# Differential attention with the scores computed once: queries on partitions, differences turned for the weighing

## The reference

```python
q1, q2 = _rope(q1, cos, sin), _rope(q2, cos, sin)    # H = 16, DH = 16
k1, k2 = _rope(k1, cos, sin), _rope(k2, cos, sin)    # KV = 4, repeated for 4 heads
s1 = einsum('bhtd,bhsd->bhts', q1, k1) * scale + mask   # causal
s2 = einsum('bhtd,bhsd->bhts', q2, k2) * scale + mask
diff = softmax(s1) - lam * softmax(s2)
out = einsum('bhts,bhsd->bhtd', diff, v)
out = (out - mean) * rsqrt(var + EPS)                # over (tokens, 32) of a head
out = (out * gn_w + gn_b).reshape(B, T, 512) * 0.8
x = layernorm(x + out @ Wo)
gate = sigmoid(max(x @ router_w.T)); e = argmax(x @ router_w.T)
y = silu_mul((gate * x) @ w_gate_up[e]) @ w_down[e] + silu_mul(x @ shared_gate_up) @ shared_down
out = layernorm(x + y)
```

## Time and profile before

| What | Value |
|---|---|
| Median of 3 runs | 820.88 us |
| The three runs | 817.32, 820.88, 823.03 us |
| Profiled execution | 814.82 us, its span 813.1 us |
| Mean granted TensorE clock | 0.964 |
| PE busy in the span | 739.4 us (91%) |
| DVE busy | 474.6 us (58%) |
| ACT busy | 316.3 us (39%) |
| POOL busy | 308.3 us (38%) |

### The profile page before, as it was taken

The page is one execution under the profiler, slowest core; times in us unless marked ns, Lnnn a source line. Parts: engine busy times, 40 slices in busy tenths (PEclk is TensorE's granted clock), DMA queues, the critical chain, the costliest instruction groups (busy, mean ns, idle before and its releaser), DMA issues.

```text
span 813.1 us, 11581 instructions
## 1 busy us (share of the span) xinstructions
PE 739.4 (91%) x4050; PEld 412.9 (51%) x4050; DVE 474.6 (58%) x1052; ACT 316.3 (39%) x584; POOL 308.3 (38%) x263
## 2 busy tenths in 40 slices
PE   7578899999989999998999999999999889999993
PEld 3343334435434444544344445444326559999993
DVE  2756987775576786437667864867325432433432
ACT  2415544354655434255454342654763102111110
POOL 4055821120885121228841211322150034666653
PEclk9879999999989999999899999999999999999997
DMA  4597084202007610120085101700020066877630
GB/s 134 126 351 184 4 191 72 41 29 42 1 26 165 108 35 30 21 46 1 27 175 75 34 29 28 220 2 0 2 85 1 27 204 218 273 266 258 226 119 0
DMA packets 55832, 78.75 MB, mean 97 GB/s; under 512 B 11543, under 2 KB 43037, under 8 KB 53920
## 3 DMA queue, kind: packets, MB, share of 16 engines
q1 hardware_dynamic: 47072, 65.02, 31.1%
q0 software_dynamic: 3824, 6.83, 2.5%
q10 hardware_dynamic: 4880, 6.16, 2.3%
HBM read 58.32 MB, written 22.41 MB: 99 GB/s over the span
## 4 chain that ended last, share of the span: by engine, by line
PE 73%; DVE 14%; DMA 4%; ACT 3%; issue 2%; POOL 2%; SPq 1%; POOLq 0%; DVEq 0%; ACTq 0%
PE pv_ps L1089 16%; PE wide_ps L1173 10%; PE wide_ps L1075 8%; PE s_ps L926 7%; DVE mneg L1506 6%; PE wide_ps L913 5%; PE wide_ps L1059 3%; PE wide_ps L1031 3%; PE s_ps L929 3%; PE s_ps L960 2%; PE misc L1184 2%; PE pv_ps L1184 2%; PE misc L1006 2%; DVE work L1536 2%; PE wide_ps L1064 2%
## 5 line engine op out<-in xcount | busy, mean ns | idle before, releaser
L1506 DVE TENSOR_REDUCE mneg<-s_ps 128x4 f32<-128x512 f32 (+2 forms) x352 | 214.7, 638 | 82.5 <-PE s_ps L926 45.7
L1287 ACT ACTIVATE w_exp<-wide_ps 128x512 f32<-128x512 f32 x320 | 179.0, 602 | 104.7 <-PE wide_ps L1075 103.3
L1089 PE MATMUL pv_ps<-w_exp,work 128*64 128x512 f32 x640 | 177.0, 633 | 1.6 <-POOL w_exp L1419 0.7
L1419 POOL TENSOR_SCALAR_AFFINE_SELECT w_exp<-w_exp 128x1024 f32<-128x1024 f32 x64 | 70.6, 1106 | 263.7 <-ACT w_exp L1287 263.4
L926 PE MATMUL s_ps<-w_exp 96*128 96x128 bf16 (+2 forms) x896 | 130.7, 250 | 22.9 <-DVE mneg L1506 13.7
L1075 PE MATMUL wide_ps<-w_exp 98*128 98x512 bf16 x320 | 122.8, 394 | 4.5 <-ACT w_exp L1287 3.3
L926 PEld LDWEIGHTS s_ps<-w_exp 96*128 96x128 bf16 x896 | 71.8, 100 | 80.3 <-DVE mneg L1506 41.8
L1075 PEld LDWEIGHTS wide_ps<-w_exp 98*128 98x128 bf16 x320 | 31.1, 100 | 141.0 <-ACT w_exp L1287 68.3
L1173 PE MATMUL wide_ps<-tables,w_exp 128*128 128x128 f32 x736 | 87.6, 278 | 0.0
L1173 PEld LDWEIGHTS wide_ps<-tables,w_exp 128*128 128x128 f32 x736 | 85.7, 195 | 0.1
L1305 ACT COPY work<-pv_ps 128x512 f32<-128x512 f32 x64 | 37.6, 588 | 67.9 <-PE pv_ps L1089 67.3
(11 more groups left out here) (162 smaller groups left out, 922.1 us busy)
## 6 DMA issues: line engine op xcount, KB each, us to landing
w_exp<-w_up_in SPq DMA_DIRECT2D x23, 1024.0 KB, 5.2
w_exp<-q_parts SPq DMA_DIRECT2D x96, 128.0 KB, 5.1
slot_tokens<-x ACTq DMA_DIRECT2D x1, 4864.0 KB, 19.4
work<-x_in SPq DMA_DIRECT2D x8, 512.0 KB, 5.3
w_exp<-w_down_in SPq DMA_DIRECT2D x8, 512.0 KB, 8.7
q_parts<-w_exp SPq DMA_DIRECT2D x6, 512.0 KB, 6.4
w_exp<-k_parts SPq DMA_DIRECT2D x18, 128.0 KB, 4.0
gated_rows<-work SPq DMA_DIRECT2D x4, 512.0 KB, 3.0
```

Of the source, the lines that this page charges most:

```text
L1089: last = nc.tensor.matmul(pv_ps[s * 64:(s + 1) * 64, :], vo[:, kt, g, :], probs[:, (b * NSTEP + n) % NP, s, :], start=(kt == 0), stop=(kt ...
L1287: nc.scalar.activation(probs[:, (b * NSTEP + n) % NP, s], st_bank(v), ACT.Exp, scale=float(DH) ** -0.5).then_inc(st_done, 1)
L1419: nc.gpsimd.affine_select(out=e, in_=e, compare_op=ALU.is_ge, fill=0.0, base=0, pattern=[[0, 8], [1, P]], channel_multiplier=-1).then_inc( ...
L1506: nc.vector.tensor_reduce(out=mneg[:, 1 - own, qt % 2, rows[0]:rows[-1] + 1], in_=s_ps[:, (v - 1) % 2, 0:len(rows) * w].rearrange("p (r k) ...
```

## The change

The scores are computed once. A batch now has 44 groups `GROUPS = (qt, r, heads, g)` in place of 40 steps: in query tile 0 a group is four heads with 128 keys each, in tile 1 two heads with 256, in tiles 2 and 3 one head with 384 and 512; each group has a bank for each of the two maps, with queries on partitions. DVE takes the maxima as before. ACT takes the exponent from the same bank, one instruction per head and map, with the row's negative maximum as bias, and the row sums as a second output (`accum_out`). DVE inverts the sums of map 2 for two groups at once, multiplies them to a `ratio`, and computes the difference of the two maps (`subtract`). PE turns the difference in blocks of 128 (`turn_diff`), ACT copies it out (`take_diff`), and `weigh` multiplies V by it, four groups beside each other in `pv_ps` with 32 rows each. The sum of map 1 is divided out at the end of each query tile (`denom` makes it, `take_out` multiplies). Maxima are no longer turned nor sent; POOL no longer zeroes the diagonal.

PSUM has seven banks in one ring each, four for scores and three for all else, and each bank has its own semaphore `freed`. A step K does the banks of group K, the difference of K - 2, the turning of K - 4, the weighing of K - 8 and the output of K - 10; the order inside a step is `PE_STEP`, `DVE_STEP`, `ACT_STEP`. The attention's output is now kept with dimensions on partitions, so mean and variance come from channel statistics (`stat`, `centre`), and `turn`, `square` and `sum` go. `x2`, the gated rows, the copy of the logits and of the shared expert's sum move from DVE to ACT (`shared_down` adds x2 on PE by an identity matmul). POOL's rotations and additions are issued as four instructions, one for each quarter of the columns. All tasks have new places in the tables. The routed experts' code is unchanged.

```diff
 NEG = -1e30
-NP = 6
+NPROB, NDIFF, NTURN = 4, 3, 6
...
+PER_BANK = [max(1, QT // (qt + 1)) for qt in range(QT)]
+GROUPS = [(qt, r, PER_BANK[qt], g) for qt in range(QT) for r in range(0, 4, PER_BANK[qt]) for g in range(KV)]
+NG, NQUAD = len(GROUPS), len(GROUPS) // KV
+FIRST_G = [min(k for k, x in enumerate(GROUPS) if x[0] == qt) for qt in range(QT)]
+LAST_G = [max(k for k, x in enumerate(GROUPS) if x[0] == qt) for qt in range(QT)]
+
+LAST_QUAD = [LAST_G[qt] // KV for qt in range(QT)]
+NALL = B * NG
+LAG_DIFF, LAG_TURN, LAG_WEIGH, LAG_OUT = 2, 4, 8, 10
...
+put(MIDDLE, 26, "mid", ("choose", 0, 1))
+put(MIDDLE, 26, "end", ("shared_gate", 0, 1))
+put(MIDDLE, 27, "mid", ("rank", 0, 1), ("ids", 0, 1))
+put(MIDDLE, 28, "mid", ("ids", 1, 1), ("ids", 2, 1), ("gate", 0, 1))
+put(MIDDLE, 28, "end", ("shared_up", 0, 1))
+put(MIDDLE, 29, "mid", ("ids", 3, 1))
...
+PE_STEP = ("bank0", "bank1", "mid", "turn", "weigh", "end")
+DVE_STEP = ("max0", "invert", "max1", "ratio", "diff", "out", "tasks")
+ACT_STEP = ("lagging", "first", "tasks", "second")
+DVE_LAG, ACT_LAG, POOL_LAG = 0, 0, 0
...
+SCORE_SLOTS, OTHER_SLOTS = (0, 1, 2, 3), (4, 5, 6)
...
-        s_ps = ctx.enter_context(nc.psum_tensor("s_ps", [P, 2, T], F32))
-        wide_ps = ctx.enter_context(nc.psum_tensor("wide_ps", [P, 4, T], F32))
-        st_ps, far = wide_ps[:, 0:RING], wide_ps[:, RING]
-        up_ps = wide_ps[:].rearrange("p (u h) t -> p u h t", u=2)
+        banks_ps = ctx.enter_context(nc.psum_tensor("banks_ps", [P, NSLOT, T], F32))
         pv_ps = ctx.enter_context(nc.psum_tensor("pv_ps", [P, T], F32))
-        misc = ctx.enter_context(nc.psum_tensor("misc", [P, T], F32))
...
+        def await_freed(engine, *use):
+
+            engine.wait_ge(freed[SLOT_OF[use]], TURN_OF[use])
+
+        def take_slot(engine, *use):
+
+            if TURN_OF[use] > 1:
+                engine.wait_ge(freed[SLOT_OF[use]], TURN_OF[use] - 1)
+            return bank_of(*use)
...
+            def score_bank(b, k, s):
+                qt, r, heads, g = GROUPS[k]
+                w = (qt + 1) * P
+                o = take_slot(pe, "bank", b, 2 * k + s)[:, 0:heads * w].rearrange("p (n k) -> p n k", k=w)
+                for n in range(heads):
+                    nc.tensor.matmul(o[:, n], q_stack[0:KROWS, qt, (2 * g + s) * 4 + r + n, :], k_stack[0:KROWS, b % 2, 2 * g + s, 0:qt + 1, :],
+                                     start=(n == 0), stop=False)
+                last = nc.tensor.matmul(o[:, :, w - P:w], identb[:], mask[:].unsqueeze(1).to_broadcast([P, heads, P]), start=False, stop=True)
+                last.then_inc(ring_full, 1)
 
...
+            def turn_diff(K):
+
+                b, k, qt, r, heads, g = group(K)
+                pe.wait_ge(diff_done, K + 1)
+                here = take_slot(pe, "turn", K, 0)
+                w = (qt + 1) * P
+                for n in range(heads):
+                    for kt in range(qt + 1):
+                        at = n * w + kt * P
+                        last = nc.tensor.transpose(here[:, at:at + P], diffs[K % NDIFF][:, at:at + P], ident[:])
+                last.then_inc(diff_turned, 1)
...
+            def weigh(J, half):
...
+                for kt in range(qt // 2 + 1) if half == 0 else range(qt // 2 + 1, qt + 1):
+                    for g in range(KV):
+                        d = turned_d[(KV * J + g) % NTURN][:, 0:heads * (qt + 1) * P].rearrange("p (n k q) -> p n k q", n=heads, k=qt + 1)
+                        last = nc.tensor.matmul(pv_ps[g * DV:(g + 1) * DV, r * P:(r + heads) * P].rearrange("p (n q) -> p n q", n=heads),
+                                                vo[:, b % 2, kt, g, :], d[:, :, kt, :], start=(kt == 0), stop=(kt == qt))
...
-            def scores(b, n, s):
-                qt, g, kt = STEPS[n]
-                v = st_at(b, n, s)
-                if s == 0 and n == FIRST_ST[qt]:
-                    pe.wait_ge(max_loaded[qt], (b + 1) * 16)
-                pe.wait_ge(st_done, v - RING)
-                gs = 2 * g + s
-                nc.tensor.matmul(st_bank(v), k_stack[0:MROWS, b % 2, gs, kt, :],
-                                 q_stack[0:MROWS, qt, gs * 4:gs * 4 + 4, :], start=True, stop=True).then_inc(st_full, 1)
...
-                for s in range(2):
-                    last = nc.tensor.matmul(pv_ps[s * 64:(s + 1) * 64, :], vo[:, kt, g, :], probs[:, (b * NSTEP + n) % NP, s, :],
-                                            start=(kt == 0), stop=(kt == qt))
-                last.then_inc(pv_step, 1)
...
+                    nc.scalar.activation(x2[:, b % 2 * QT + arg], y[:, arg % 2], ACT.Identity, scale=rstd[:, arg % 2:arg % 2 + 1],
+                                         bias=centre_y[:, arg % 2:arg % 2 + 1]).then_inc(x2_done, 1)
...
-                        nc.scalar.activation(probs[:, (b * NSTEP + n) % NP, s], st_bank(v), ACT.Exp, scale=float(DH) ** -0.5).then_inc(st_done, 1)
...
+            def exponents(K, s):
+
+                b, k, qt, r, heads, g = group(K)
+                w = (qt + 1) * P
+                if K >= NPROB and s == 0:
+                    act.wait_ge(diff_done, K - NPROB + 1)
+                act.wait_ge(max_done, 2 * K + s + 1)
+                here = bank_of("bank", b, 2 * k + s)
+                for n in range(heads):
+                    ins = nc.scalar.activation(probs[:, K % NPROB, s, n * w:(n + 1) * w], here[:, n * w:(n + 1) * w], ACT.Exp,
+                                               bias=mneg[:, (2 * K + s) % 6, n:n + 1], scale=1.0,
+                                               accum_out=(total2[:, K // 2 % 2, K % 2, n:n + 1] if s else total1[:, qt % 2, g, r + n:r + n + 1]))
...
+            def take_diff(K):
...
+                nc.scalar.copy(turned_d[K % NTURN][:, 0:w], bank_of("turn", K, 0)[:, 0:w]).then_inc(freed_by("turn", K, 0), 1)
...
-                ins = prepare(nc.gpsimd, what, pair, rot, ALL)
+                for q in range(QT):
+                    ins = prepare(nc.gpsimd, what, pair, rot, slice(q, q + 1))
...
-                        nc.gpsimd.affine_select(out=e, in_=e, compare_op=ALU.is_ge, fill=0.0, base=0,
-                                                pattern=[[0, 8], [1, P]], channel_multiplier=-1).then_inc(diag_done, 1)
...
-                elif name == "norm":
-                    qt, g = divmod(arg, KV)
-                    dve.wait_ge(near_full, v)
-                    t = misc[:].rearrange("p (r s d) -> p r s d", r=4, s=2)
-                    c.link(nc.vector.reciprocal(rl[:], t[:, :, :, DV]))
-                    nc.vector.tensor_tensor(o12[:], t[:, :, :, 0:DV], rl[:].unsqueeze(3).to_broadcast([P, 4, 2, DV]), ALU.mult).then_inc(near_done, 1)
-                    dve.wait_ge(near_done, v)
-                    c.link(nc.vector.scalar_tensor_tensor(att[:, qt, g * 4:g * 4 + 4, :], o12[:, :, 1], neglam[:], o12[:, :, 0],
-                                                          ALU.mult, ALU.add))
...
+            def invert(K):
+
+                b, k, qt, r, heads, g = group(K)
+                pair = K // 2 % 2
+                await_freed(dve, "bank", b, 2 * k + 3)
+                nc.vector.reciprocal(inv2[:, pair, :, 0:heads], total2[:, pair, :, 0:heads]).then_inc(sums_inverted, 1)
...
+            def compare(K):
...
+                nc.vector.scalar_tensor_tensor(ratio[:, pair, :, 0:heads], total1[:, qt % 2, g:g + 2, r:r + heads], neglam[:],
+                                               inv2[:, pair, :, 0:heads], ALU.mult, ALU.mult).then_inc(ratio_ready, 1)
...
+            def subtract(K):
...
+                for n in range(heads):
+                    here = slice(n * w, (n + 1) * w)
+                    ins = nc.vector.scalar_tensor_tensor(diffs[K % NDIFF][:, here], probs[:, K % NPROB, 1, here], ratio[:, pair, K % 2, n:n + 1],
+                                                         probs[:, K % NPROB, 0, here], ALU.mult, ALU.add)
+                ins.then_inc(diff_done, 1)
...
+            def take_out(b, qt):
...
+                nc.vector.tensor_tensor(oT[:, :, qt * P:(qt + 1) * P], pv_ps[:].rearrange("p (r t) -> p r t", r=4),
+                                        denomT.rearrange("p (r t) -> p r t", r=4), ALU.mult).then_inc(out_taken, 1)
```

1122 lines of the change are left out of this document (514 added, 608 removed).

## The result

The changed kernel takes 767.27 us (median of 4 runs, 765.08 to 768.74) against 819.1 us before in the same comparison: ratio 0.9363, with a 95% interval of 0.9311 to 0.9416. The forecast was 792 us with a range of 740 to 860: the sign and the range were right, the gain was 52 us where 29 had been forecast. The profiled execution's span went from 813.1 to 764.6 us, 48.5 us less.

A forecast was written before the change was run, and what follows sets the result against it. TensorE was taken to bound the kernel before; after, PE, ACT and DVE at 113, 121 and 119 us a batch. Tile maxima gave 501 us, with waits 531 against 562.4; tail +3, so 28 less: 787 profiled, 792 median, range 740 to 860.

The forecast's parts named there:

- PE's terms: TensorE in a middle batch: computing scores once, cheaper weighing, added transposes and denominators leave 113 us busy.
- The first way to the sum: TensorE per middle batch, removed and added work netted from line prices: 43 us less, to about 106 us.
- The count by columns: All the new kernel's matmuls priced by columns, 0.23 us per four passes of 128: 113 us, the dearer estimate, taken.
- ACT's terms: ScalarE in a middle batch: 128 exponents with bias and row sum, 44 copies and more tasks, from 72 to about 121 us.
- DVE's terms: VectorE in a middle batch: maxima stay, norm goes, 64 differences come; 113 us, 119 with waits for POOL.
- POOL's share: A third of VectorE's 64 differences wait 0.3 us for quartered rotations: 6 us a batch.
- The sum: Largest engine of each query tile added: 135.5 us a middle batch, 501 in all, times 1.06 for waits is 531.
- The signs: Trace figures named beforehand as confirming or refuting, such as PE 75 to 85% busy, ACT over 80%, in middle batches.
- ACT is cheap: Rival on ScalarE's exponents: the row sum costs nothing, 746 us in the profile, 752 us; chance 0.18.
- TensorE's clock: Rival: TensorE, less busy, runs half of query tile 3's work at 1.2 GHz; 822 us, no change; chance 0.17.
- ACT becomes the bound: Rival: dearer exponents without overlap make middle batches need 154 us, kernel slower, 876 us as median; chance 0.25.

The follow-up runs named there:

- three masks: The changed kernel with each score bank's mask added three times on PE, same result: 775.53 us, ratio 0.9483.

## Why the prediction was right in sign and range, and short in size

**PE's terms.** PE is at 122 us and not 113. The first way to the sum (106) read its prices wrongly: it took the busy time of a line as what goes when the line goes. But a matmul's record overlaps with the next one's: in the earlier trace rows a matmul of the second computing (L1075) lasts 0.38 us and the next one starts 0.22 us after it. Counted from each start to the next, the second computing took 20.0 us of batch 1 and not 31.3, the old weighing 42.3 and not 45.5. Counted so in the kernel after, the new weighing is 13.1 us (16 forecast), the denominators are 4.1 (8 forecast), and the 160 transposes are 23.9 (17.2 forecast). The price of these, 0.43 us for four, was that of one place at full clock; the 64 transposes of batch 1 before took 7.6 us, 0.48 for four. The score banks were rightly taken as unchanged: 29.3 us with their mask before, 29.5 after. The count by columns, which gave 113, had 59 us for the 44 groups and 54 for the tasks; from start to start the groups are 66.5 us, most of the excess being the transposes, and the tasks 55. PE's busy time fell by 27 us in batch 1, not by 36 or 43.

The lines alone would mislead here. The mask (L861, before L929) has the same columns in both kernels, in 88 instructions after and 32 before, and its busy time seems to double. First before, then after:

```profile
188.00:343.60 155.60, 12.20 (x32) 3.11 (x32) 0.98 0.27 53
152.60:293.80 141.20, 22.68 (x88) 9.05 (x88) 0.90 0.28 57
```

From start to start it is 8.3 us before and 10.0 after.

**ACT's terms.** 121 forecast, 112.4 measured. From start to start the exponents with their sums take 66.9 us (72 forecast), the copies 21.4 (21), the tasks 24 (26 to 29). The row sum was sized nearly right (0.08, forecast 0.10). The profile does show the second instruction that the text named as a sign of error ("It is wrong if ACT shows a second instruction of 0.2 us per exponent"); this sign was badly chosen, since the read overlaps with the exponents on both sides. The Trainium skill (VectorE: DVE Perf Modes, section on two Vector instructions with no wait between them) describes such a pair for VectorE, and here the trace shows one on ScalarE, with a net cost of a third of its duration.

**DVE's terms.** 119 forecast, 111.3 measured. From start to start the maxima take 48.2 us (56 forecast, by their durations), the differences 36.8 (37.3 with POOL's share), all else 26 (26). The lock with POOL was right in mechanism: undoing the portions made the kernel 16 us slower, as expected, by differences of up to 1.67 us in the mean of a group. The portions by themselves are no gain, as the run on the kernel before shows.

**The sum: two errors that cancelled in part.** "I take the largest engine of each tile of a middle batch" can be done again with measured busy times. Windows of batch 1, cut where PE begins the score banks of query tiles 0 to 3:

```profile
149.20:164.60 15.40, 14.71 (x120) 10.14 (x121) 10.69 (x25) 14.08 (x63) 0.00 (x0) 0.89 0.35 54
164.60:189.50 24.90, 22.59 (x205) 14.05 (x203) 21.88 (x58) 22.79 (x86) 9.31 (x16) 0.95 0.00 1
189.50:242.10 52.60, 40.98 (x294) 26.50 (x294) 41.91 (x107) 40.72 (x116) 35.64 (x58) 0.76 0.05 16
242.10:291.70 49.60, 44.90 (x338) 26.50 (x336) 38.11 (x79) 35.85 (x92) 12.97 (x16) 1.00 0.67 131
```

The largest of PE, DVE and ACT in each add up to 124.3 us, where 135.5 had been forecast. In the four batches it is 99, 124, 125 and 104 us, 452 in all, against 501: the loads were 49 us too high, in the middle batches mostly on ACT in query tiles 0 and 1 (22.8 us in tile 1, where 28.8 had been forecast), in the others mostly in query tile 3 (31.8 for 37.9 in batch 0). Adding by tiles did little harm itself, as 124.3 is near the 121.9 of the busiest engine of the whole batch. The waits were too low: the batches take 1.08, 1.15, 1.14 and 1.10 times these sums, where 1.06 was added for all, from batches 1 and 3 before (the earlier trace rows has 1.11 for batch 0). That makes 506 us where 531 were forecast. The small error of the middle batches (144 forecast, 141.2 and 142.4 measured) is luck: there both errors were of one size. Batches 0 and 3, whose waits are fewer, show what is left of the loads' error (117 and 127 forecast, 109.6 and 113.0 measured).

From the forecast to the result: 787 us in the profile, less 7.4 for batch 0, 14 for batch 3 and 4.4 for the middle ones, and 3.7 more for the tail (6.7 longer, forecast 3), is 765; the profiled execution took 766.4. The last 5 us of the forecast's 792 were added because the median had stood 0.74% above the profiled run; this time it stands 0.1% above.

**The signs.** Two of the signs of being wrong came although the forecast held: the second instruction, and a clock below 0.9 in a whole batch (0.87 in batch 0). Of the other figures, PE's busy share of a middle batch is 86% (75 to 85 named) and ACT's 80%.

**The rivals.** *ACT is cheap* (752 us) was half right: a row sum is not free, but without any the kernel takes 755.5. *TensorE's clock* did come: 0.87 to 0.92 in all batches, and in the stretch of rotations of batch 1 it was 0.76, with PE busy 39.5 of 50 us:

```profile
190.00:240.00 50.00, 39.48 (x285) 25.85 (x283) 39.51 (x97) 38.47 (x110) 35.64 (x58) 0.76 0.04 12
```

In batch 0 it cost nothing that shows: with three masks it ran at 0.97 and was no shorter. For the middle batches no run tells, as there the three masks add work and clock at once. *ACT becomes the bound* did not come: ACT is busy 80% of a middle batch of 141 us, not the bound of one of 154, though a microsecond taken off it is worth more once the maxima are gone.

**What bounds the changed kernel** is no single engine, but three loaded ones that wait for each other in fixed orders, with the four score banks between them. Taking load off ACT alone gave 12 us, off DVE alone 33, off both 56, adding 55 to PE cost 8, one bank less cost 57 with unchanged loads, and two other orders on ACT cost some 20. That the ring of banks matters is shown. That it is the main bound is not: with four banks a fifth of them stands free in the mean, and the orders that released banks earlier were slower. What a fifth bank would give back was not tried.

**Where the 52 us come from.** From computing the scores once, which takes 27 us of a middle batch off PE, with four banks in the loop. 35 us of it lie in batch 0, which no longer makes the next batch's maxima. The portions (16 us) and the small tasks on ACT (7, not clear of noise) help to keep that gain, and are worth nothing or less by themselves. They aren't terms that add up with it.

## What to carry to other kernels

Take the price of an instruction from its start to the next one's start, not from its duration or its line's busy time. Here 31.3 us of a line were 20.0 us of the engine. When work moves from one bounded engine to three balanced ones, ask for the coupling beside the loads: how far one engine may run ahead, and what stands behind a wait in its order. No formula came out of these runs for it: a batch was 1.14 to 1.17 times its busiest engine with four banks, and one bank less took the whole gain. And try an edit such as cutting an engine's instructions into portions on the kernel that it is meant for: the same edit was worth 16 us in one kernel and cost some 14 in the other, where PE waited for what was queued behind it.

## What the runs showed of the hardware that I had not expected

- An exponent with a row sum on ScalarE is two instructions, the exponent (690 ns for 512 columns) and a read of the sum (244 ns in the mean), which overlap to 0.68 us from start to start; the sum's net cost is 0.08 us.
- Adding 14 us of matmul to batch 0 raised PE's busy time by only 6.6 us, while its granted clock went from 0.87 to 0.97; in batch 1 it was 10.2 us, with the clock from 0.90 to 0.94.
- Six differences of 384 columns on VectorE, with both inputs in SBUF, took 1.67 us in the mean beside whole rotations on GpSimd, 0.84 beside portions; with no GpSimd work beside it one took 0.62.
- A matmul's record on TensorE is longer than what it costs: 0.38 us for 512 columns of bf16, with the next one starting 0.22 us after it. The busy times of PE's lines in one batch add up to 184 us where the engine was busy 122.
